# Feeding the input of a block kernel by token tile between its first attention slots, with the start's transfers and the rotary tables cut up

## What is computed

```python
x  = L0_attn_x
xn = _layernorm(x, axis=-1)
x  = x + _L0_attn_ref(xn, ...) + _L0_ffn_ref(xn, ...)
```

```python
q = l2norm(q) * qs;  k = l2norm(k) * ksc
q = q * cos * scale + rotate_half(q) * sin * scale
k = k * cos / scale + rotate_half(k) * sin / scale
```

## Time and profile before

| | |
|---|---|
| three runs | 973.52, 974.99 (median), 976.41 us |
| profiled execution | 971.3 us, span 969.5 us |
| busy shares | PE 89%, PEld 60%, DVE 65%, ACT 72%, POOL 65% |
| mean granted clock of TensorE | 0.983 |
| transfers | 13.47 MB, nearly all of what is read at the start in the first fortieths of the span |

### The profile page before, as it was taken

The page is one execution under the profiler, slowest core; times in us unless marked ns, Lnnn a source line. Parts: engine busy times, 40 slices in busy tenths (PEclk is TensorE's granted clock), DMA queues, the critical chain, the costliest instruction groups (busy, mean ns, idle before and its releaser), DMA issues.

```text
span 969.5 us, 26414 instructions
## 1 busy us (share of the span) xinstructions
PE 862.3 (89%) x10836; PEld 580.5 (60%) x10836; DVE 634.5 (65%) x1082; ACT 701.7 (72%) x1449; POOL 631.0 (65%) x500
## 2 busy tenths in 40 slices
PE   0678889989899898998999989999999999999876
PEld 0345666666667666666566656565656565656552
DVE  5874666666667567576575776757575758575632
ACT  0446786977868779677797778787878787878651
POOL 4588677675876758667586665757575758585700
PEclk9979999999999999999999999999999999999997
DMA  9100000000000000000000000000000000000000
GB/s 295 30 1 3 1 2 2 3 3 2 2 3 1 3 1 1 3 2 3 1 2 3 1 2 2 1 21 4 17 7 23 2 23 2 21 3 24 1 23 11
DMA packets 20482, 13.47 MB, mean 14 GB/s; under 512 B 4579, under 2 KB 19597, under 8 KB 20237
## 3 DMA queue, kind: packets, MB, share of 16 engines
q1 hardware_dynamic: 15108, 10.49, 3.6%
q10 hardware_dynamic: 5256, 1.31, 0.7%
HBM read 9.70 MB, written 2.10 MB: 12 GB/s over the span
## 4 chain that ended last, share of the span: by engine, by line
PE 63%; ACT 15%; DVE 10%; issue 7%; POOL 3%; DMA 1%; DVEq 0%; POOLq 0%; SPq 0%; ACTq 0%
PE pQK L1181 8%; PE pS L1108 6%; PE pT L1093 5%; PE pT L1050 5%; PE pM L1125 5%; PE pV L1146 4%; PE pS L1082 4%; PE pM L1254 4%; DVE m L734 4%; PE pT L1237 3%; PE pQK L1345 3%; PE pM L1119 2%; PE pS L1069 2%; ACT prT L545 2%; ACT pr L598 1%
## 5 line engine op out<-in xcount | busy, mean ns | idle before, releaser
L366 POOL TENSOR_TENSOR rn<-rn,half_neg 128x16 f32<-128x16 f32 x64 | 187.5, 2929 | 5.3
L379 POOL TENSOR_TENSOR m<-m 128x1024 f32<-128x1024 f32 x64 | 150.9, 2358 | 0.0
L364 POOL TENSOR_SCALAR rn<-ss 128x16 f32<-128x16 f32 x64 | 16.3, 254 | 193.3 <-DVE ss L747 192.1
L386 POOL TENSOR_TENSOR qkn<-m,rn 128x1024 f32<-128x1024 f32 x64 | 121.7, 1902 | 5.0
L1181 PE MATMUL pQK<-wqkv,hT 128*128 128x512 f32 x256 | 123.6, 606 | 0.9 <-DVE m L734 0.9
L780 DVE TENSOR_REDUCE mx<-pS 128x8 f32<-128x1024 f32 x64 | 78.1, 1220 | 63.8 <-PE pS L1082 63.8
L561 ACT ACTIVATE sq<-pQK 128x1024 f32<-128x1024 f32 x64 | 65.4, 1022 | 25.5 <-PE pQK L1181 25.4
L747 DVE TENSOR_REDUCE ss<-sq 128x16 f32<-128x1024 f32 x64 | 77.6, 1213 | 6.7 <-ACT sq L561 6.4
L782 DVE TENSOR_TENSOR pr<-pS,mx 128x1024 f32<-128x1024 f32 x64 | 78.4, 1225 | 2.2
L521 ACT ACTIVATE kT<-pT 128x512 f32<-128x512 f32 x64 | 38.0, 595 | 57.3 <-PE pT L1050 56.8
L545 ACT ACTIVATE prT<-pT 128x1024 f32<-128x1024 f32 x64 | 65.0, 1016 | 15.6 <-PE pT L1093 14.8
(11 more groups left out here) (169 smaller groups left out, 2015.9 us busy)
## 6 DMA issues: line engine op xcount, KB each, us to landing
x<-in_L_attn_x SPq DMA_DIRECT2D x4, 512.0 KB, 9.4
xs<-in_L_attn_x SPq DMA_DIRECT2D x8, 256.0 KB, 2.8
out<-aqkT SPq DMA_DIRECT2D x8, 256.0 KB, 2.2
wqkv<-in_L_ffn_wqkv SPq DMA_DIRECT2D x2, 768.0 KB, 9.8
tab<-in_k_tab SPq DMA_DIRECT2D x1, 1024.0 KB, 10.4
w<-in_L_ffn_w SPq DMA_DIRECT2D x2, 341.0 KB, 10.5
wo<-in_L_ffn_wo SPq DMA_DIRECT2D x2, 256.0 KB
cst<-in_k_cst ACTq DMA_DIRECT2D x1, 404.5 KB, 4.3
```

Source lines behind the costliest of these rows:

```text
L366: eng.tensor_tensor(rn[:, k % 2, :], rn[:, k % 2, :], half_neg[:, 0:2 * H], ALU.pow).then_inc(S["rn_done"], 1)
L379: eng.tensor_tensor(m1[:, k % 2, :], m1[:, k % 2, :], m2[:, :], ALU.add).then_inc(S["add_done"], 1)
L386: eng.tensor_tensor(qkn[:, k % 2, :].rearrange("p (h d) -> p h d", d=DH), m1[:, k % 2, :].rearrange("p (h d) -> p h d", d=DH), rn[:, k % 2 ...
```

## The change

The start before the bodies is dissolved. Its work is done by a function `feed(k)` on each engine, which stands before slot k of the first step.

- **Transfers.** x is loaded in 8 transfers of one token tile of all batches (256 KB each). SP issues tiles 0 and 1, the first layer's `wqkv`, the table of tile 0 alone (128 KB), then tiles 2 to 7, the ten columns, `w1`, the eight `b1c` transfers, the rest of the table, and the other weights. ACT issues the constants, the gains, the mask and the retention weights.
- **Feeding.** Slot 0 of the first step needs only token tile 0. Tiles 0 and 1 are normalised, turned and evicted ahead of slot 0, tiles 2 and 3 ahead of slot 1, tiles 4 to 7 ahead of slot 2. POOL's power is cut into five parts (`PAIRS`). The transposes go to the halves of `pS`, and `xn` is an alias of a half of `pr`.
- **Group norm.** The channel statistics go in halves into DVE's `feed(2)`; the group norm's later part, with the bias additions, goes into `feed(3)`. PE's and POOL's parts of it move into slot 3. The turning of the retention weights and `bias_through_w1` stand in PE's `feed(2)`.
- **Tables.** `rope_part` multiplies the tables with the gains in parts: tile 0 ahead of slot 0, tiles 1 to 7 in POOL's `feed(3)`, the second layer's q and k tables before slot 3 of steps (0, 1) and (0, 2). Gains get a buffer of their own.

```diff
+        PAIRS = (slice(0, 1), slice(1, 2), slice(2, 4), slice(4, 6), slice(6, 8))
+        FEED = ((0, 1), (2, 3), (4, 5, 6, 7))
...
-            for b in range(NB):
-                sp.dma_start(x[:, b, :, :], a["L0_attn_x"][b].rearrange("(t p) d -> p t d", p=P)).then_inc(x_ld[b], 16)
-            sp.dma_start(tab[:, :, :, :], a["k_tab"]).then_inc(tab_ld, 16)
+            def load_tile(t):
+                sp.dma_start(x[:, :, t, :], x_steps[t]).then_inc(x_ld[t], 16)
...
+            load_tile(0)
+            load_tile(1)
             sp.dma_start(wqkv[:, 0, :], a["L0_ffn_wqkv"][0]).then_inc(wqkv_ld, 16)
+            sp.dma_start(tab[:, 0, :, :], a["k_tab"][:, 0, :, :]).then_inc(tab_ld, 16)
+            for t in range(2, NT):
+                load_tile(t)
+            for name, arg in (("ng", "norm_g"), ("nb", "norm_b"), ("ob", "ob"), ("fg", "ffn_norm_g"),
...
+            column("b1a", a["L0_attn_b1"].rearrange("(c p) -> p c", p=P), 2)
...
             for l in range(DEPTH):
                 sp.dma_start(w1[:, l, :], a["L0_ffn_w1"][l]).then_inc(w1_ld, 16)
+            with nc.allow_non_contiguous_dma(reason="one value per partition"):
...
+            sp.dma_start(tab[:, 1:NT, :, :], a["k_tab"][:, 1:NT, :, :]).then_inc(tab_rest_ld, 16)
             sp.dma_start(wqkv[:, 1, :], a["L0_ffn_wqkv"][1]).then_inc(w_ld, 16)
...
-            for half in range(2):
-                steps = slice(half * NT // 2, (half + 1) * NT // 2)
+            def scale_of(i):
+                steps = PAIRS[i]
...
-                eng.wait_ge(var_done, half + 1)
+                eng.wait_ge(var_done, i + 1)
...
-            eng.wait_ge(tab_ld, 16)
-            eng.wait_ge(gain_ld, 16 * 4)
-            for l in range(DEPTH):
-                for g in range(2):
...
+            def rope_part(l, steps, gs=range(2)):
+                size = steps.stop - steps.start
+                for g in gs:
+                    eng.tensor_tensor(rope[l][:, steps, g, :], tab[:, steps, g, :],
+                                      gain[:, l, g, :].unsqueeze(1).broadcast_to([P, size, DH]),
                                       ALU.mult).then_inc(rope_done, 1)
                     for s in range(2):
...
+            def feed(k):
+                if k == 0:
+                    scale_of(0)
+                    eng.wait_ge(tab_ld, 16)
+                    eng.wait_ge(gain_ld, 16 * 4)
+                    rope_part(0, slice(0, 1))
+                    scale_of(1)
+                    scale_of(2)
+                elif k < 3:
+                    scale_of(k + 2)
+                else:
+                    pool_group_norm(eng, 0)
+                    eng.wait_ge(tab_rest_ld, 16)
+                    rope_part(0, slice(1, NT))
 
             def body(new, old, ff):
                 for k in range(NB):
-                    if k == 1 and new and is_start(new):
-                        pool_group_norm(eng, 0)
+                    if new and is_start(new):
+                        feed(k)
+                    if new in ((0, 1), (0, 2)) and k == NB - 1:
+                        eng.wait_ge(LS["qkn_done"], NB)
+                        rope_part(1, slice(0, NT), (new[1] - 1,))
...
-            if k == NB - 1 and new and new[0] == 0:
-                if is_start(new):
-                    eng.wait_ge(gn[0]["done"], 1)
+            if k == NB - 1 and new and new[0] == 0 and not is_start(new):
                 act_retention_in(eng, new[1])
...
             if k == NB - 1 and new and new[0] == 0:
+                if is_start(new):
+                    eng.wait_ge(gn[0]["done"], 1)
+                    act_retention_in(eng, 0)
                 act_retention_project(eng, new[1], 0)
...
-            eng.dma_start(mask32, a["k_mask"]).then_inc(cst_ld, 16)
+            for g, n in enumerate(("q_scale", "k_scale")):
+                for l in range(DEPTH):
+                    eng.dma_start(gain[:, l, g, :], a["L0_ffn_" + n][l:l + 1, :].broadcast_to([P, DH])).then_inc(gain_ld, 16)
+            eng.dma_start(mask32, a["k_mask"]).then_inc(mask_ld, 16)
...
-            def column(name, ap, k=1):
-                with nc.allow_non_contiguous_dma(reason="one value per partition"):
...
+            def feed(k):
+                for t in FEED[k]:
                     eng.wait_ge(xnt_mm, t + 1)
-                    eng.activation(xnT[:, :, bass.ds(t * P + 1, P)], xn_banks[u][:, :].rearrange("p (b n) -> p b n", b=NB),
+                    eng.activation(xnT[:, :, t * P + 1:t * P + 1 + P], xn_banks[t % 2].rearrange("p (b n) -> p b n", b=NB),
                                    ACT.Copy).then_inc(xnt_ev, 1)
+                if k == 0:
+                    eng.wait_ge(xnt_ev, 1)
+                if k == 2:
+                    for g in range(2):
+                        eng.wait_ge(awt_mm, g + 1)
+                        eng.activation(aT[:, 4 * g:4 * g + 4, :], pT[:, 512 * g:512 * g + 512].rearrange("p (k n) -> p k n", k=4),
+                                       ACT.Copy).then_inc(awt_ev, 1)
+
...
-            for b in range(NB):
-                eng.wait_ge(x_ld[b], 16)
...
+            def tile_stats(t):
+                eng.wait_ge(x_ld[t], 16)
+                for b in range(NB):
+                    eng.bn_stats(xst[:, b, t, :], x[:, b, t, :]).then_inc(xst_done, 1)
+                eng.wait_ge(xst_done, NB * t + NB)
                 for b in range(NB):
                     eng.bn_aggr(mv[:, t, b, :], xst[:, b, t, :]).then_inc(st_done, 1)
...
+            def normalize(t):
+                eng.wait_ge(rstd_done, 1 + [t in range(p.start, p.stop) for p in PAIRS].index(True))
+                need(eng, xnt_mm, t - 1)
...
+            def feed(k):
+                if k == 0:
+                    tile_stats(0)
+                    tile_stats(1)
+                    normalize(0)
+                    tile_stats(2)
+                    normalize(1)
+                    tile_stats(3)
+                    eng.wait_ge(cst_ld, 16)
+                    eng.wait_ge(mask_ld, 16)
+                    eng.tensor_copy(mask16[:, :], mask32).then_inc(mask_done, 1)
+                    eng.wait_ge(rope_done, 6)
+                elif k == 1:
+                    normalize(2)
+                    tile_stats(4)
+                    normalize(3)
+                    tile_stats(5)
+                elif k == 2:
+                    normalize(4)
+                    tile_stats(6)
+                    normalize(5)
+                    tile_stats(7)
+                    input_stats(0)
+                    normalize(6)
+                    normalize(7)
+                    input_stats(1)
+                    dve_group_stats(eng, 0)
+                else:
+                    bias_into_ffn()
+                    dve_group_spread(eng, 0)
+                    dve_group_scale(eng, 0, c("ng"), c("nb"))
...
+            def input_stats(h):
+
+                eng.wait_ge(xnt_ev, NT // 2 * (h + 1))
+                for b in range(NB):
+                    eng.bn_stats(cbst[0][:, b, h, :], xnT[:, b, 1 + h * T // 2:1 + (h + 1) * T // 2]).then_inc(cs_done, 1)
+                if h:
+                    eng.wait_ge(cs_done, NB * 2)
...
                     if new and is_start(new):
-                        if k == 0:
-                            input_stats()
-                        if k == 1:
-                            bias_into_ffn()
-                            dve_group_norm(eng, 0, c("ng"), c("nb"))
+                        feed(k)
+                    if new == (0, 1) and k == 0:
+                        eng.wait_ge(rope_done, 12)
+                    if new == (1, 0) and k == 0:
+                        eng.wait_ge(rope_done, 18)
...
             if k == NB - 1 and new and new[0] == 0:
+                if is_start(new):
+                    eng.wait_ge(be_done, 3)
+                    pe_group_norm(eng, 0)
                 pe_retention_project(eng, new[1], 0)
...
-            eng.wait_ge(cst_ld, 32)
-            eng.wait_ge(aw_ld, 16 * 6)
...
+            def turn_weights_in():
+                eng.wait_ge(aw_ld, 16 * 6)
+                for g in range(2):
...
+            def feed(k):
+                for t in FEED[k]:
                     eng.wait_ge(xn_done, 4 * t + 4)
                     need(eng, xnt_ev, t - 1)
...
+                if k == 0:
+                    eng.wait_ge(wqkv_ld, 16)
+                if k == 2:
+                    turn_weights_in()
+                    bias_through_w1()
+                    eng.wait_ge(xnt_ev, NT)
+                    eng.wait_ge(awt_ev, 2)
+                    eng.wait_ge(w_ld, 16 * (1 + 3 * DEPTH))
...
-                    if new and is_start(new) and k == 1:
-                        bias_through_w1()
-                    if new and is_start(new) and k == 2:
-                        eng.wait_ge(be_done, 3)
-                        pe_group_norm(eng, 0)
-                        eng.wait_ge(w_ld, 16 * (1 + 3 * DEPTH))
+                    if new and is_start(new) and k < NB - 1:
```

(22 more changed lines are left out.)

87 lines of the change are left out of this document (21 added, 66 removed).

## The result

The kernel before took 974.47 us (median of 4 runs, 973.52 to 976.41), the changed one 990.70 (4 runs, 986.07 to 995.13): ratio 1.0164, 95% interval 1.0114 to 1.0213. It is slower, by 16 us. The forecast was 988, range 977 to 996. The profiled execution took 989.89 us, span 988.1, against 971.3 and 969.5.

What follows compares the result with a forecast made beforehand. The prediction took PE's chain from the second step on as the bound, so only the first step's hand-over and work added inside steps count: 9.6 late plus 3.6 is 13.2, giving 988 us, range 977 to 996.

Steps and rivals of the forecast that it cites:

- Feed 0: Work ahead of slot 0: DVE is free of slot 0's products at 27.1, slot 0 24 us ahead of before.
- Feeds 1 and 2: Tile work ahead of slots 1 and 2: the lead goes, POOL ends slot 2 at 77.3 against 75.1.
- The slow normalisations: Ahead of slots 1 and 2: normalisations of tiles 3 and 5 beside POOL's work, four at 0.62, 2.5 us per tile.
- the loop: Other possible cause of the slow normalisations, removed by the change; if it held, the sum would be 2.9 less.
- The hand-over: From POOL's slot 2 to ACT's turned q and k: 86.1 against 77.37, 8.7 late, 9.6 with half the pause's cost.
- these products: POOL's table products for tiles 1 to 7 at the hand-over: 4.7 us beside the path, costing nothing on top.
- The pause: PE idle some 7 us ahead of the retention projection; a dropped clock would cost 1.8, half taken, 0.9.
- Steps (0, 1) and (0, 2): Second layer's table products ahead of the retention's power: each step loses 1.8, together 3.6, between nothing and 5.3.
- The subtraction of 0.84: In each of the two steps, 0.84 taken off 2.66, since PE takes the result 0.84 after DVE has it.
- The early start: Rival: DVE's tile work fits its waits, POOL ends slot 2 at 50.4, 13.7 faster, 961; chance 0.11.
- The rival of a full clock in the start: Rival: PE at full clock in the start saves some 10 us, giving 978; chance 0.14.

Runs made afterwards that it cites:

- experiment 1: Changed kernel with the second layer's table products of steps (0, 1) and (0, 2) moved behind POOL's retention part: 986.12 us, ratio 1.0137.
- experiment 3: Changed kernel with the group norm's later half and the bias additions moved ahead of slot 2's scores: 986.02 us, ratio 1.0130.
- experiment 4: As experiment 3, with the table products of tiles 1 to 7 also moved behind POOL's retention part of the first step: 989.69 us, ratio 1.0163.
- Experiment 8: Changed kernel with the edits of experiment 1 and experiment 2 together: 982.37 us, ratio 1.0091.
- experiment 6: Kernel before with only the rotary tables in parts, layer 0's rest behind all 32 normalisations, layer 1's as in experiment 1: 968.18 us, ratio 0.9949.
- experiment 2: Changed kernel with ScalarE's wait for the bias additions and columns moved behind slot 3 of the first step: 989.85 us, ratio 1.0185.
- experiment 7: Changed kernel with all tiles ahead of slot 0, group norm, biases and retention input placed as before, layer 1's tables as in experiment 1: 962.30 us, ratio 0.9891.
- experiment 11: As experiment 10, with the q half of layer 1's table computed ahead of slot 0: 958.92 us, ratio 0.9877.
- experiment 9: As experiment 7, with GpSimd's layer 0 table products for tiles 1 to 7 waiting for all 32 normalisations: 959.80 us, ratio 0.9881.
- experiment 10: As experiment 9, with the input's group norm split and PE's average moved right behind slot 0: 957.29 us, ratio 0.9844.

## Why the prediction was right, and where it was off

The mechanism came as forecast: slot 0 far ahead, the lead gone by slot 2, then a late hand-over and two longer steps. The closeness of the number is in part luck. By the profiles the change costs 18.6 us where 13.2 were forecast: 4.4 more at the hand-over, 3.2 more in steps (0, 1) and (0, 2), some 2 given back behind them. The median came out nearer than the profile (990.7 against 988, but 989.9 against 984.5) only since the profiled execution lay 0.8 us under its median and not 3.7 as before.

- **Feed 0, right.** The small products took 1.44 (1.6 forecast) and waited for a gain transfer, not for the table, until 11.4 (11.1); tile 1's normalisation starts at 14.4 (14.1), slot 0's sum ends at 25.8 (24.8), since q and k took 3.6 there, not 2.9.
- **Feeds 1 and 2, right in the sum, with errors that cancel.** Sums of squares at 41.3 (40.5) and 69.2 (69.7), GpSimd's slot 2 at 76.9 (77.3). The weights and biases stand ahead of slot 2 with 1.92 and 2.53, as costed. The two slow groups of normalisations took 1.3 us more each. Against it, slot 1 went from its projection to the end of its sum in 6.3, not 7.1, and from the turning of slot 0's q and k to the end of slot 2's q and k matmuls passed 6.7, not 7.9; the turning took 1.07 instead of 1.94. In experiments 1, 3, 4 and 8 the slower biases took this gain back.
- **The slow normalisations: right cause, size off.** Four took 3.84 us, not 2.5. The term was a mean per instruction; what counts is how long GpSimd's instructions beside them last: the first two waited out the addition and the scaling, and the last two were fast (experiment 6). Nothing of it is the loop: in the changed kernel there is none, and in experiment 6 the looped ones are fast. The Trainium skill (GPSIMD Engine Reference, 1. Specifications) states that GpSimd shares its SBUF interfaces with VectorE. The trace agrees with it beside products, additions and scalings; beside GpSimd's powers eight normalisations still took 2.14.
- **The hand-over: mechanism right, the term too small** (9.6 forecast, 14.0 measured). Slot 2's end gave back 0.4. *"Behind slot 2's scaling POOL now has the group norm's power"*: it didn't follow at once. ScalarE stands at the wait for the biases ahead of its slot 3 (3.65 idle, to 72.69); DVE had moved these behind slot 2's work. So PE's scores start only at 73.88 and its average, queued behind them and the turn, at 77.91: 2.4 us, shown by experiment 2. *"three small operations, 0.23 each with waits 0.7"*: they took 1.09, 0.57 and 0.58, each to the end of one of the first three table products. The prediction costed these products at nothing, and they cost 1.6. The pause cost 0.84 on the projection and 1.46 on q and k, and from the projection's start to the turned q and k 7.0 us passed where 6.1 were forecast with half the pause's price: 0.9. The Trainium skill (TensorE: Matmul & The Clock Gate, Part 1) holds that the array runs at 1.2 GHz by default and after idling, and by that rule the whole 1.8 is paid. The rows agree with it rather than with the half: PE's last work ended at 78.3, and the granted clock was 0.97 from 80 to 82 and 0.50 from 82 to 86.
- **Steps (0, 1) and (0, 2): too small** (1.8 each forecast, 3.75 and 3.1 measured). The subtraction of 0.84 was wrong: DVE's wait grew by the whole 2.6, and 1.1 more followed in (0, 1). Experiment 8 takes the tables away: 60.35 to 55.8, 64.2 to 61.8. The 4.5 in (0, 1) is more than the 3.75 by which the step grew; the rest wasn't traced.
- **The rivals.** The early start did not survive; experiment 7 shows what it needs, no tile work between the slots. The rival of a full clock in the start didn't come: 0.50 from 28 to 34 and 0.60 from 41 to 57.

## What to carry to other kernels

Work that is put between the links of a relay isn't hidden by the relay's idle time when each engine runs its instructions in order. Here it used up a lead of 23 us within two slots. Cut the tables and transfers by tile, let them run as one stream ahead of the relay, and keep GpSimd's elementwise work off the time in which VectorE is on the path. Where they must overlap, price a VectorE instruction by the GpSimd instruction that it may have to wait for, not by a mean. When a step moves, list every wait of every engine that stands behind its result: here the unlisted one (ScalarE's, for the biases) cost as much as the clock. And before a trace is compared with another, compare the stretch ahead of the edit: here identical instructions differed by 2 us.

## What the runs showed of the hardware

- Some DVE instructions wait for the elementwise instruction that GpSimd is running, to its end. Beside the normalisations above, a 128x4 scale took 1.09 us instead of 0.23 and ended at 81.37, GpSimd's product at 81.35; one of the group norm in experiment 11 took 1.76 instead of 0.17 and ended at 46.23, GpSimd's scaling at 46.20. GpSimd's powers did not hold them, and the channel statistics took 4.83 beside products in experiment 7 and 4.84 beside none before.
- GpSimd's power costs by column: 0.71 us for 2, 1.04 for 4, 1.67 for 8 and 2.93 for 16. Cutting two of 16 into five pieces (two of 4, three of 8) cost 7.1 us against 5.9.
- In experiment 9 slot 0's q and k took 3.62 us from 34.31 though the windows from 34 to 38 show a granted clock of 1.00, and 1.88 in experiment 10 with the same 1.00. The granted clock of a short window doesn't tell alone how fast a matmul ran.
